# A depthwise convolution's running sum moved from SBUF to two PSUM banks

## The reference

```python
def _L2_conv_ref(x, w_dw, w_pw):
    C = x.shape[1]
    u_dw, s_dw = _quant_per_channel_dw(w_dw)
    y = lax.conv_general_dilated(x, _ste(w_dw, u_dw), window_strides=(1, 1), padding=((1, 1), (1, 1)), dimension_numbers=DN, feature_group_count=C)
    y = y / s_dw
    u_pw, s_pw = _quant_global(w_pw)
    y = lax.conv_general_dilated(y, _ste(w_pw, u_pw), window_strides=(1, 1), padding=((0, 0), (0, 0)), dimension_numbers=DN)
    y = y / s_pw
    return y
```

## Time and profile before

| | |
|---|---|
| median of three runs | 417.78 us (417.62 to 448.15) |
| the profiled execution's own time | 419.33 us |
| its span | 416.8 us |
| busy: PE, DVE, ACT, POOL | 379.1, 314.7, 244.1, 200.3 us |
| mean granted clock of PE | 0.982 of full |
| DVE taps of L1368 | 32 instructions, 29.9 us |

### The profile page before, as it was taken

The page is one execution under the profiler, slowest core; times in us unless marked ns, Lnnn a source line. Parts: engine busy times, 40 slices in busy tenths (PEclk is TensorE's granted clock), DMA queues, the critical chain, the costliest instruction groups (busy, mean ns, idle before and its releaser), DMA issues.

```text
span 416.8 us, 13469 instructions
## 1 busy us (share of the span) xinstructions
PE 379.1 (91%) x4953; PEld 275.6 (66%) x4953; DVE 314.7 (75%) x718; ACT 244.1 (59%) x571; POOL 200.3 (48%) x331
## 2 busy tenths in 40 slices
PE   4699999999999999999999999999998999958773
PEld 1588788888878777678777777877776433324441
DVE  3757878777788677978877777778879499856883
ACT  5235566666656555656565566665567355458871
POOL 6564657575767445343444344444444343433331
PEclk9999999999999999999999999999999999988996
DMA  8400000000000000000000000000000000000112
GB/s 187 97 4 4 3 2 0 0 0 0 2 2 3 2 2 2 2 2 2 3 2 0 0 0 0 0 2 0 2 4 2 0 1 0 2 0 19 40 39 57
DMA packets 8343, 5.06 MB, mean 12 GB/s; under 512 B 4874, under 2 KB 8074, under 8 KB 8306
## 3 DMA queue, kind: packets, MB, share of 16 engines
q1 hardware_dynamic: 7456, 4.43, 4.5%
q10 hardware_dynamic: 850, 0.12, 0.2%
HBM read 2.98 MB, written 1.57 MB: 11 GB/s over the span
## 4 chain that ended last, share of the span: by engine, by line
PE 59%; DVE 21%; issue 11%; POOL 5%; ACT 2%; POOLq 0%; DVEq 0%; ACTq 0%
PE bank L860 11%; PE bank L889 10%; PE bank L826 10%; PE bank L869 9%; PE bank L836 6%; DVE conv L1368 6%; PE bank L918 3%; PE bank L933 3%; DVE row_max L1065 3%; POOL y_out L1567 2%; DVE v L1024 2%; DVE stats L681 2%; PE bank L549 2%; PE bank L935 1%; PE bank L1476 1%
## 5 line engine op out<-in xcount | busy, mean ns | idle before, releaser
L1103 POOL TENSOR_TENSOR probs<-probs,row_max 128x384 f32<-128x384 f32 x128 | 105.3, 829 | 118.6 <-DVE row_max L1065 117.7
L967 ACT ACTIVATE probsT<-bank 128x384 f32<-128x384 f32 x128 | 61.1, 492 | 76.2 <-PE bank L869 76.2
L1061 DVE TENSOR_TENSOR probs<-bank,bias 128x384 f32<-128x384 f32 x128 | 65.3, 552 | 52.6 <-PE bank L860 52.3
L1065 DVE TENSOR_REDUCE row_max<-probs 128x6 f32<-128x384 f32 x128 | 68.3, 545 | 1.0
L869 PE MATMUL bank<-cst,probs 128*128 128x128 f32 x384 | 62.9, 281 | 0.0
L889 PE MATMUL bank<-v,probsT 128*64 128x18 f32 (+1 forms) x1536 | 57.7, 219 | 3.5 <-DVE headsN L1090 3.2
L889 PEld LDWEIGHTS bank<-v,probsT 128*64 128x64 f32 x1536 | 50.2, 137 | 15.0 <-issue 13.1
L860 PE MATMUL bank<-k,q 64*64 64x128 f32 x1536 | 58.0, 282 | 1.9 <-ACT k L1012 1.9
L860 PEld LDWEIGHTS bank<-k,q 64*64 64x64 f32 x1536 | 42.3, 135 | 21.8 <-issue 20.8
L1012 ACT ACTIVATE k<-bank,cst 128x256 f32<-128x256 f32 x128 | 54.0, 483 | 0.0
L869 PEld LDWEIGHTS bank<-cst,probs 128*128 128x128 f32 x384 | 44.7, 141 | 11.0 <-issue 5.0
(11 more groups left out here) (142 smaller groups left out, 549.2 us busy)
## 6 DMA issues: line engine op xcount, KB each, us to landing
x<-in_x SPq DMA_DIRECT2D x4, 384.0 KB, 7.3
out_dram<-y_out SPq DMA_DIRECT2D x8, 192.0 KB, 2.1
w<-in_L_conv_w_qkv SPq DMA_DIRECT2D x1, 432.0 KB, 4.9
cst<-in_consts SPq DMA_DIRECT2D x1, 304.0 KB, 5.8
p<-in_L_conv_w_out SPq DMA_DIRECT2D x1, 144.0 KB, 4.6
pos<-in_L_conv_pos_emb SPq DMA_DIRECT2D x8, 2.0 KB
cst<-in_consts SPq DMA_DIRECT2D x1, 117.0 KB, 3.5
w_raw<-in_L_conv_qkv_w ACTq DMA_DIRECT2D x1, 108.0 KB, 5.4
```

What stands on the lines that cost most here:

```text
L967: nc.scalar.activation(probsT[w][:, :], ps_probsT[w % 2][:, 0:NP * 128], ACT.Exp).then_inc(L.s.probsT_sb, 1)
L1061: nc.vector.tensor_tensor(out, scores, b, ALU.add).then_inc(L.s.biased, 1)
L1065: nc.vector.tensor_reduce(row_max[w][:, :], probs[w][:, :, :], AX.X, ALU.max).then_inc(L.s.maxed, 1)
L1103: nc.gpsimd.tensor_tensor(probs[w][:, :, :], probs[w][:, :, :], by_row(row_max[w]), ALU.subtract).then_inc(L.s.shifted, 1)
```

## The change

The running sum no longer lives in `conv[par]`. ACT writes the first tap into a view of bank 5 or 6 (`ps_sum[par]`), DVE's first three taps read and write that bank, and the fourth reads it and writes `conv[par]` in SBUF, where PE finds it as before. The waits follow: ACT's first tap waits until the taps of pair `j - 2` have left the bank, instead of for the pointwise of that pair, and for pair 1 also for the last evacuation of layer 1's products from the bank; the fourth DVE tap waits for the pointwise of pair `j - 2`, which reads `conv[par]`.

```diff
+        ps_sum = [b[0:C, :].rearrange("c (y x) -> c y x", x=SIDE) for b in bank[5:7]]
+
         def act_first_tap(act, j, par):
 
             act.wait_ge(l2_norm, j * 2 + 2)
-            wait(act, l2_pw, j - 1)
-            nc.scalar.activation(conv[par][:, :, :], tap_of(par, 0), ACT.Copy, scale=dw_u[:, 0:1]).then_inc(l2_first, 1)
+            wait(act, l2_tap, (j - 1) * DVE_TAPS)
+            if j == 1:
+                evacuated(act, L1, B - 1, L1.v_index(1))
+            nc.scalar.activation(ps_sum[par], tap_of(par, 0), ACT.Copy, scale=dw_u[:, 0:1]).then_inc(l2_first, 1)
 
         def dve_depthwise(dve, j, par, i0=0, i1=DVE_TAPS):
 
             if i0 == 0:
                 dve.wait_ge(l2_first, j + 1)
-            y = conv[par][:, :, :]
             for i in range(i0, i1):
                 if i:
                     dve.wait_ge(l2_tap, j * DVE_TAPS + i)
-                nc.vector.scalar_tensor_tensor(y, tap_of(par, 1 + i), dw_u[:, 1 + i:2 + i], y,
+                if i == DVE_TAPS - 1:
+                    wait(dve, l2_pw, j - 1)
+                y = conv[par][:, :, :] if i == DVE_TAPS - 1 else ps_sum[par]
+                nc.vector.scalar_tensor_tensor(y, tap_of(par, 1 + i), dw_u[:, 1 + i:2 + i], ps_sum[par],
                                                ALU.mult, ALU.add).then_inc(l2_tap, 1)
```

## The result

The changed kernel takes **414.42 us** (median of 22 runs, 412.18 to 417.39) against 417.79 for the kernel before (22 runs, two of them outliers of 448.15 and 1988.78). The ratio of the runs is 0.9932, with a 95% interval of 0.9909 to 0.9954: 2.8 us less, a gain that is small but clear of the scatter. The profiled execution has a span of 413.9 us against 416.8.

What follows compares the result with a forecast made beforehand. DVE was taken to bound layer 2, with PE right behind. Profiled execution 419.33 - 3.1 = 416.2 us, lying 1.55 above the median, so 417.78 becomes 414.7; range 414 to 415.5, or 412.6 to 416.9 with (c) and nearer (b).

Steps and rivals of the forecast that it cites:

- The size: Whole kernel: 3.1 us gained on the path through layer 2, median from 417.78 to 414.7 us.
- The long tap: Layer 2 DVE taps: with the sum from PSUM no long tap beside POOL's add, DVE 5.6 us lighter.
- rival (a): Layer 2: POOL holds any DVE instruction reading SBUF, the tap stays at 1.66 us, time 417.8; chance 0.07.
- PE next in line: Layer 2: PE becomes the bound with a period of 4.30 us, pointwise 7 at 359.11 instead of 362.09.
- The swallowed 2.5 us: Layer 2: of DVE's 5.6 us saved, 2.5 become idle time behind PE's own period.
- The others keep up: Layer 2: ACT has 2.1 us spare, and norm steps and POOL's adds are ready before PE needs them.
- What a tap costs with PSUM: Layer 2 DVE taps through PSUM: 0.75 us each; PE stays the bound below 0.86 us.
- The upper end, 0.89: Layer 2 DVE tap at most 0.75 + 0.14 = 0.89 us, where 0.7 of the gain is lost.
- Rival (b): Layer 2: PSUM write, landing and read slow the taps; chance 0.03 beyond 0.98 us, 0.08 for 0.86 to 0.98.
- The waits: Layer 2: ACT's and DVE's new waits are already met, and nothing queues behind any of them.
- The clock in layer 3: Layer 3: PE's low-clock stretch and the idle stretch before it kept as they are, layer 3 as long as before.
- Rival (c): Layer 3: PE's clock stays up, 412.7 to 413.7 us, or stays low longer, 415.7 to 416.7; chance 0.10, split evenly.

Runs made afterwards that it cites:

- The experiments on POOL: Kernel before, POOL's layer 2 residual add cut to one column (414.7 us), made a copy (416.25 us), or made a memset (one execution, 417.01 us).
- the copy: Kernel before with POOL's layer 2 residual add replaced by a copy with one SBUF input: 416.25 us, ratio 0.9943.
- Both runs with a PE tap left out: One of PE's four taps left out for pairs 2 to 7: in the kernel before 418.65 us, in the changed kernel 412.22 us.
- the changed kernel with the lighter PE: Changed kernel with one of PE's four taps left out for pairs 2 to 7: 412.22 us, ratio 0.986 to the kernel before.
- the last versions: Changed kernel with taps moved from PE to DVE in some pairs, four lists: 411.95, 412.19, 411.32 and, in one run, 415.83 us.
- the one with POOL's short add: Kernel before, sum in SBUF, with POOL's layer 2 residual add on 1 column of 512: 414.7 us, ratio 0.9917.
- the version with 7 and 6 taps: Changed kernel with 7 taps on DVE for pair 0 and 6 for pair 1, instead of 4: 412.19 us, ratio 0.983.

## Why the prediction was right

- **The size.** 414.7 us was forecast and 414.42 measured; 3.1 us of gain, and 2.8 by the ratio, 2.9 by the spans. That the medians meet within 0.3 us is partly luck, since single runs lie anywhere from 412.18 to 417.39; the stretches of the trace are the better test. There layer 3 starts 363.03 - 360.08 = 2.95 us earlier, where 3.07 was forecast. The difference is made of 0.17 by which pointwise 1 came later in this execution (333.14 against 332.97), and which the forecast could not know, less 0.05 of rounding.
- **The long tap.** It was read from one coincidence in the timeline and from L1090, and it holds: all PSUM taps lie within 0.733 to 0.753 although `pad` is still read from SBUF and POOL still reads two tensors, so rival (a) is out. The experiments on POOL show the cause itself, which the trace of before could only suggest. I had written that both instructions read two tensors; for POOL one is enough, as the copy shows.
- **PE next in line.** Forecast: a period of 4.30 us, and 359.11 - 332.97 = 26.14 from pointwise 1 to 7. Measured: 4.29 and 26.09. The forecast's own terms, 0.85 + 3.44, add up to 4.29; it rounded them to 4.30, and five times that is the 0.05. Both runs with a PE tap left out confirm it, one from each side.
- **The swallowed 2.5 us.** Measured as 2.63, from the changed kernel with the lighter PE.
- **The others keep up.** No wait of PE for DVE, ACT or POOL is left in layer 2. The norm matmul behind pointwise 5 was forecast at 351.2, with DVE ready at 349.7; it came at 351.33, and DVE's last step before it ended at 349.88. One detail was wrong: I expected gaps of about 0.6 us of DVE in every pair, ended by ACT's first tap. Only one such wait is in the trace, 0.52 us at 345.29. In the pairs with norm steps DVE is busy for 4.25 of 4.46 us and falls behind ACT, and it catches up only in the pairs behind. Its taps end at 356.73 + 0.74 = 357.47, 1.8 us ahead of PE, which is the spare time that the last versions ran into.
- **What a tap costs with PSUM.** 0.75 taken, 0.752 measured. The upper end, 0.89, was far off, and so was the estimate by the Trainium skill, VectorE: DVE Perf Modes, the section on the TRN2 errata, which gave 65 ns more for a tap: the measured step differs by 0.004 us from that in SBUF, and the measurement decides. Rival (b) is out with it.
- **The waits.** Neither of the two new ones ended an idle time in the trace.
- **The clock in layer 3** fell in the same place, behind the same idle stretch: the granted clock was 0.50 from 373 to 376 us before and is 0.50 from 370 to 373 now. Layer 3 took as long as before: 416.8 - 363.03 = 53.8 us and 413.9 - 360.08 = 53.8. Rival (c) did not occur in this pair of profiles, but the low stretch is shorter in others, below.

## What to carry to other kernels

Where an instruction of DVE with two SBUF inputs is sometimes twice as long as its median, look at what POOL reads at that moment. Taking one input from PSUM cured it here; a POOL instruction that read less, or nothing, did so too. Before crediting the saving, work out the period that the engine standing right behind needs by itself, from the spacing of its instructions in a stretch where it does not wait: the gain ends there, here at 3 of 5.6 us. The rest is then to be had only by moving work to the engine that became free, and only where it is free.

## What the runs showed of the hardware

The runs of one kernel scatter by 5 us (412.18 to 417.39), as much as the change is worth and more. There is one trace for each kernel, but for the first 300 us all of them run the same code, so their traces can be laid beside each other. Two places differ. The first is the start: matmuls that run slowly at first take their short time from some 28 us on in one trace and from some 36 us on in another. The same instructions, in the timelines of PE of the changed kernel and of the one with POOL's short add:

```profile
28.73 1.49 PE L563 MATMUL bank<-pos,cst 64*128 64x64 f32 x6
30.15 0.39 PE L565 MATMUL bank<-cst,p_raw 96*96 96x96 f32 x1
30.47 1.56 PE L860 MATMUL bank<-k,q 64*64 64x128 f32 x24
```

```profile
28.28 0.85 PE L563 MATMUL bank<-pos,cst 64*128 64x64 f32 x6
29.06 0.29 PE L565 MATMUL bank<-cst,p_raw 96*96 96x96 f32 x1
29.28 0.89 PE L860 MATMUL bank<-k,q 64*64 64x128 f32 x24
```

The next group of L860 starts at 34.14 in the one and 31.87 in the other, and the same 2.3 us still lie between them at pointwise 1, 333.14 against 330.86; the stretch behind it is 26.09 us in both. That PE's clock is what differs at the start is not shown: the profile gives a granted clock of 1.00 on both sides of the step.

The second place is the fall of the clock in layer 3. Counted from 7 us behind the first matmul of layer 3, the granted clock in four stretches of 3 us is 0.70, 0.50, 0.67 and 1.00 in the changed kernel and 1.00, 0.70, 0.73 and 1.00 in the version with 7 and 6 taps, whose layer 3 is the same code. From that matmul to the end of the span it is 53.8 us in the first and 409.2 - 356.87 = 52.3 in the second. So for an effect below 1% here the stretches inside the trace are the sharper measure, and the runs only confirm it.

A last figure: the ACT instruction that writes PSUM takes 0.687 us, the same one into SBUF 0.72.
